# A transformer's step loop: ScalarE makes the reciprocal lengths between two copies, and VectorE gates ahead of its sums of squares

## The chip, the cores and the metric

The kernel runs on one core of a Trainium2 chip. The core has five engines with their own in-order queues: TensorE (PE), VectorE (DVE), ScalarE (ACT), GpSimd (POOL) and SyncE (SP), which here only issues transfers. They meet by semaphores. The metric is the device time in microseconds (us) of one execution; the median of three runs is 2576.67 us (2573.55 to 2577.73).

## The reference, cut to what matters

The input x is 2048 tokens of width 128, all in float32. Two layers follow each other:

- layer 0 adds to x a causal attention of 16 heads and a mixture of 8 experts (two are picked for each token), both on the normalised x;
- layer 1 adds to the result a state space branch (a short convolution, rates, and a scan over the tokens with 16 states for each of 256 channels) and a branch of six transformer layers, both on the normalised x.

The change lies in the six transformer layers. Each computes, on tokens shifted by one in half of the channels:

```
q, k, v = split(x @ Wqkv)                    # 16 heads of 64
q = q / max(|q|, 1e-12) * q_scale            # the lengths: one per token and head
k = k / max(|k|, 1e-12) * k_scale
q, k = rotary(q), rotary(k)
x = x + softmax(mask(8 q k^T)) v @ Wo        # windows of 32, each sees itself and the one before
xn = (x - mean) / sqrt(var + 1e-5) * g + b
a, gate = split(xn @ W1 + b1)                # 341 wide each
x = x + (a * gelu(gate)) @ W2 + b2
```

## The kernel before

After layer 0 the core goes through one loop of 96 steps (6 transformer layers of 16 tiles of 128 tokens, `NTILE` = 96), software-pipelined over all layers, with seven steps more to drain it. Each engine has its own function with its own copy of the loop (`transformer_pe`, `transformer_act`, `transformer_dve`, `transformer_pool`, `transformer_sp`), and the order inside a step is written out by hand. The values are never formed: the heads' probabilities weigh the rows of x (the "mixed values"), and one product with the folded Wv Wo follows.

What happens to one tile runs over several steps. In step n:

- TensorE projects q and k of tile n+2 (L1447), forms the attention output of tile n-1 (L1550, from both halves of the mixed values), turns q and k rows of tile n+1 (L1455), does a third of a feed-forward product (L1564, L1565) or a product down (L1571) and four transposes (L1556), the scores of tile n+1 (L1471, L1462) in two halves with the mixing of tile n between them (L1512).
- ScalarE (`transformer_act`) copies the two halves of the mixed values of tile n-1 out of PSUM (`mix_out`, L1785), squares q and k of tile n+2 (L1729), takes the 16 exponentials of tile n (L1778), copies turned x, q and k (L1739, L1757, L1765, L1767), makes the decays of the scan (L472), and then gelu for a third of four tiles' hidden rows (`gelu`, L1800), between two loads of its function tables (L1903, L1913). Last it makes the reciprocal lengths of tile n+2: logarithm L1718 and exponential L1722 (`lengths`), which wait for VectorE's clamped sums (semaphore `squares`).
- VectorE (`transformer_dve`) takes the maxima of tile n (`top`, L1932), the rotary products of tile n+2 (`rotate`, L1952, one for q and one for k), the sum of tile n-1 (L1969), the softmax weights (L1936, L1938, L1940) and their transpose (L1944), then sums the squares of tile n+2 (`sum_squares`, L1958) and clamps them (L1962), does its share of the convolution in steps 4 to 14 (L1182), the gate (`gated`, L2018: the product of one PSUM bank with gelu's output), and the scan (L2034).
- GpSimd (`transformer_pool`) refines the reciprocal lengths by a Newton step (`better`, L2126 to L2132), scales q and k of tile n+1 by them (`normal`, L2139), does the scan's inputs and outputs (L481, L509, L511) and the rotary additions of tile n+2 (L2119, L2120); in one of four steps also the layer norm of four tiles (L2143 to L2151).

`forward_step` sets what the feed-forward does: steps with n % 4 = 3, 0, 1 have the first, second and third part of the product up with gelu and gate; steps with n % 4 = 2 have none, but the transposes and the product down. The scan's 64 later units are in four blocks of 16 steps: steps 23 to 38, 41 to 56, 59 to 74 and 77 to 92 (a unit's decay and scan are issued at the end of the step before).

PSUM's eight banks are four pairs. `pair_table` hands them on in a ring: q of tile n+3 goes to the pair of step n's feed-forward part, which is free when the gate has read it (semaphore `hv`), k of tile n+3 to the pair of the first half of the mixed values (`mixT`, first copy), and the attention output of step n+1 to the pair of the second half.

Of the kernel before, what the change touches and what calls it, by code (L numbers as in the profile page):

```python
# [41 lines left out]
NTILE = L * NT  # L42
# [1107 lines left out]
def variance_dve(k):  # L1150

    V, s, st = k.ve, k.sem, k.st[:, :, 0:NTH]
    V.wait_ge(s("ln_squared"), 1)
    V.tensor_reduce(st[:, 2, :], k.sqr, X_AXIS, ALU.add).then_inc(s("v"), k.v.up())
    V.wait_ge(s("v"), k.v.n)
    V.tensor_scalar(st[:, 3, :], st[:, 2, :], 1.0 / P, EPS, ALU.mult, ALU.add).then_inc(s("v"), k.v.up())
    V.wait_ge(s("v"), k.v.n)
    V.reciprocal(st[:, 0, :], st[:, 3, :]).then_inc(s("v"), k.v.up())
    V.wait_ge(s("v"), k.v.n)
    V.tensor_scalar(st[:, 2, :], st[:, 0, :], -EPS, 1.0 + EPS, ALU.mult, ALU.add).then_inc(s("ln_var"), 1)  # L1160
# [89 lines left out]
def forward_step(n):  # L1250

    what = (("up1", 8), ("up2", 9), ("turn_normal", 6), ("up0", 7))[n % 4]
    m = (n - what[1]) // 4
    return (what[0], m) if 0 <= m < NTILE // 4 else (None, m)
# [450 lines left out]
def transformer_act(k):  # L1705
    A, s, ps = k.ac, k.sem, k.ps

    def pair(*key):
        p = k.pair[key]
        return ps[:, 2 * p:2 * p + 2, :]  # L1710
# [4 lines left out]
    def lengths(n):  # L1715

        A.wait_ge(s("squares"), n + 1)
        A.activation(k.lnx[:], k.sx[:, n % 2, :], ACT.Ln, scale=65536.0).then_inc(s("lnx"), 1)  # L1718
        A.wait_ge(s("lnx"), n + 1)
        if n >= 2:  # L1720
            A.wait_ge(s("normal_k"), n - 1)
        A.activation(k.rn[:, n % 2, :], k.lnx[:], ACT.Exp, scale=-0.5, bias=k.ln256[:]).then_inc(s("rn"), 1)  # L1722

    def square(what, n):
        w = 0 if what == "q" else 1
        A.wait_ge(s(what + "_mm"), n + 1)
        if n:
            A.wait_ge(s("summed"), n)
        A.activation(k.sq[:, w, :], flat(what, n), ACT.Square).then_inc(s("sq_" + what), 1)  # L1729
# [51 lines left out]
    def mix_out(n, i):  # L1781
        A.wait_ge(s("mixed"), 2 * n + i + 1)
        if n:
            A.wait_ge(s("fin_mm"), n)
        A.activation(k.mixT[:, :, 2 * i:2 * i + 2, :].rearrange("p c w q -> p w c q"), pair(f"mix{i}", n).rearrange("p w (c q) -> p w c q", q=WIN), ACT.Copy).then_inc(s("mixT"), 1)  # L1785
# [20 lines left out]
    def norm_squared():  # L1806
        A.wait_ge(s("ln_centred"), 1)
        A.activation(k.sqr, k.xn[:, NTH:NT, :], ACT.Square).then_inc(s("ln_squared"), 1)
# [54 lines left out]
    for n in range(LAST_STEP):  # L1863
        if 1 <= n <= NTILE:
            mix_out(n - 1, 0)
            mix_out(n - 1, 1)
        if n + 2 < NTILE:
            square("q", n + 2)
            square("k", n + 2)
        if n < NTILE:  # L1870
            probs(n, 0)
            probs(n, 1)
        if n == 0:
            norm_squared()
        if n + 3 < NTILE:
            turned_input(n + 3)
        if n in FOLD_STEPS:
            folded_share(n)
        for u in units(n):
            if u // NS + 1 < NCH:  # L1880
                unit_state(k, u)
        if new_frame(n + 1) and n + 1 < NTILE:
            halo_turned(n + 1)
        if n + 1 < NTILE:
            queries_out(n + 1)
            keys_out(n + 1)
        for u in units(n + 1):
            A.wait_ge(s("chunk"), 32 * (u // NS - NCH // 2 + 1))
            unit_decay(k, u)
        if n in IN_LATE:  # L1890
            projected_in("late", n, IN_LATE[n])
        if n == FACTOR_STEP:
            factors(n)
        if n in RATE_STEPS:
            rates(n, RATE_STEPS[n])
        for place, l, half in FOLDS.get(n, ()):
            folded(place, n, l, half)
        what, m = forward_step(n)
        if what == "turn_normal":
            normal_turned(m)  # L1900
        elif what:
            if n < NTILE:
                A.preload_act_table_set("gelu_and_others")  # L1903
            gelu(m, int(what[2]))
        if n == HAT_STEP:
            turned_hat(0)
            turned_hat(1)
        if n in IN_EXTRA:
            projected_in("extra", n, IN_EXTRA[n])
        if n in SILU_STEPS:  # L1910
            convolved(SILU_STEPS[n])
        if what and what != "turn_normal" and n < NTILE - 1 or IN_EXTRA.get(n, 0) >= ET:
            A.preload_act_table_set("natural_log_exp_and_others")  # L1913
        if n + 2 < NTILE:
            lengths(n + 2)
        if n in RATE_STEPS:
            softplus(RATE_STEPS[n])


def transformer_dve(k):  # L1920
# [94 lines left out]
    def gated(m, j):  # L2015
        o, w = FCH[j]
        V.wait_ge(s("gelu"), 3 * m + j + 1)
        V.scalar_tensor_tensor(k.hv[0:w, j, :], pair("extra", 4 * m + 7 + j)[0:w, 1, :], k.colA[0:w, m // (NT // 4) % 2, 5 + j:6 + j], k.hv[0:w, j, :], ALU.add, ALU.mult).then_inc(s("hv"), 1)  # L2018
# [26 lines left out]
    for n in range(LAST_STEP):  # L2045
        taps = conv_share(n)
        for a, t in taps[:2]:
            conv_dve(k, a, t)
        if n < NTILE:
            top(n)  # L2050
        if n == 0:
            centre_dve(k)
        if n + 2 < NTILE:
            rotate("q", n + 2)
            rotate("k", n + 2)
        if 1 <= n <= NTILE:
            finish(n - 1)
        if n in CHUNK_OUT:
            chunk_sum(CHUNK_OUT[n])
        if n < NTILE:  # L2060
            weigh(n)
        if n == 0:
            variance_dve(k)
        if n + 2 < NTILE:
            sum_squares(n + 2)
        for a, t in taps[2:]:
            conv_dve(k, a, t)
        if n == 1:
            normal_dve(k)
            V.wait_ge(s("turned"), TURNED + 2)  # L2070
            V.memset(k.hv[DH:DH + WIN, 2, :], 1.0)
            V.tensor_copy(k.xs[:, NTH + 1:NT + 1, :], k.xn[:, NTH:NT, :]).then_inc(s("copied"), 1)
        what, m = forward_step(n)
        if what and what != "turn_normal":
            gated(m, int(what[2]))
        if n == NTILE + 6:
            down_last()
        elif n % 4 == 2 and m >= 1:
            down(m - 1)
        if n % 4 == 1 and 0 <= (n - 5) // 4 < NTILE // 4:  # L2080
            measure((n - 5) // 4)
        if n == NTILE + 1:
            normalise_last()
        if n == NTILE + 3:
            add_last()
        elif n == NTILE + 4:
            add_layer(0)
            add_layer(1)
        elif n == NTILE + 5:
            add_layer(2)  # L2090
        for u in units(n + 1):
            scan(u)
# [343 lines left out]
```

## Time and profile before

| What | Value |
|---|---|
| median of three runs | 2576.67 us |
| profiled execution | 2573.51 us, its span 2571.7 us |
| PE busy | 2374.6 us (92% of the span) |
| DVE busy | 2266.8 us (88%) |
| POOL busy | 1949.9 us (76%) |
| ACT busy | 1851.5 us (72%) |
| mean granted TensorE clock | 0.981 |
| the step loop | step 0 begins at 953 us, the last exponential of a tile at 2531 us |

The profile is one execution on the chip. Busy time counts work instructions of an engine, not its waits. Times in the rows are microseconds from the span's start; in groups of instructions "mean ns" is nanoseconds. The slices of the page show TensorE's granted clock at nine tenths or more of full speed throughout.

### The profile page before, as it was taken

The numbers are of one execution on the slowest core, as the hardware profiler recorded it, in microseconds if no ns is written. First come the engines' busy times: TensorE is split into PE (matmuls) and PEld (weight loads), VectorE is DVE, ScalarE is ACT, GpSimd is POOL, SyncE is SP. The second block draws the span as 40 slices with busy tenths as digits, with TensorE's granted clock in tenths as the row PEclk, the third lists the DMA queues.
The fourth block names the chain that finished last, engine by engine and source line by source line (L and its number), as shares of the span: only waits on it lengthen the run. The fifth ranks groups of instructions, "written<-read, shape, count | busy, mean of one in ns | idle before, by whom it ended". The sixth has DMA issues, their size and how long they took to land. (4 is left out here: it accounts for less than half of the span.)

```text
span 2571.7 us, 67534 instructions
## 1 busy us (share of the span) xinstructions
PE 2374.6 (92%) x26742; PEld 1428.9 (56%) x26742; DVE 2266.8 (88%) x2520; ACT 1851.5 (72%) x4113; POOL 1949.9 (76%) x1768
## 2 busy tenths in 40 slices
PE   7999999899898869899889999999999999999997
PEld 4444443333333336566566666666667666666665
DVE  6778879879999988999769999899999999899994
ACT  4566555556666647777778888888888888888883
POOL 2441147947888857777578999899999999999991
PEclk9999999999999989999999999999999999999999
DMA  3000000002333310300211112111211221111101
GB/s 109 9 9 11 9 7 7 15 24 57 57 60 57 62 33 8 98 14 12 67 44 43 32 51 46 40 35 49 46 40 30 45 59 33 37 35 33 30 17 40
DMA packets 171112, 97.22 MB, mean 38 GB/s; under 512 B 97156, under 2 KB 167792, under 8 KB 169264
## 3 DMA queue, kind: packets, MB, share of 16 engines
q1 hardware_dynamic: 170799, 92.91, 15.9%
q8 instruction: 215, 3.52, 0.6%
q14 instruction: 98, 0.79, 0.1%
HBM read 66.91 MB, written 7.08 MB: 29 GB/s over the span
## 5 line engine op out<-in xcount | busy, mean ns | idle before, releaser
L608 PE MATMUL ps<-xnT,qp 128*128 128x512 f32 (+3 forms) x1280 | 564.5, 562 | 11.2 <-ACT prob L833 11.1
L833 ACT ACTIVATE prob<-ps,mneg,shift 128x1024 f32<-128x1024 f32 (+7 forms) x384 | 366.6, 955 | 285.1 <-DVE mneg L728 284.6
L1952 DVE TENSOR_TENSOR area<-ps,tab 128x2048 f32<-128x2048 f32 x192 | 430.7, 2284 | 59.1 <-ACT area L1729 33.7
L728 DVE TENSOR_REDUCE mneg<-ps 128x1 f32<-128x1024 f32 (+7 forms) x384 | 340.7, 888 | 73.2 <-PE ps L608 72.8
L1447 PE MATMUL ps<-wqk,area 128*128 128x512 f32 x768 | 360.8, 613 | 28.3 <-DVE area L2018 23.4
L736 DVE STREAM_TRANSPOSE area<-prob 128x1024 f32<-128x1024 f32 (+7 forms) x384 | 352.1, 917 | 31.1 <-ACT prob L833 24.9
L2139 POOL TENSOR_TENSOR area<-area,rn 128x1024 f32<-128x1024 f32 x192 | 371.6, 1957 | 7.5
L1550 PE MATMUL ps<-wvo,area 128*128 128x128 f32 x3072 | 364.4, 277 | 3.3 <-ACT area L1785 3.3
L1550 PEld LDWEIGHTS ps<-wvo,area 128*128 128x128 f32 x3072 | 354.8, 193 | 22.3 <-issue 13.1
L608 PEld LDWEIGHTS ps<-xnT,qp 128*128 128x128 f32 x1280 | 222.8, 196 | 202.9 <-issue 175.3
L1778 ACT ACTIVATE ps<-ps,nmxl 128x64 f32<-128x64 f32 x1536 | 322.5, 344 | 4.1 <-DVE nmxl L1932 4.0
L1729 ACT ACTIVATE area<-ps 128x1024 f32<-128x1024 f32 x192 | 196.7, 1025 | 103.3 <-PE ps L1447 103.2
L956 POOL TENSOR_TENSOR vb<-staged,own 128x1024 f32<-128x1024 f32 x48 | 90.9, 1894 | 226.7 <-PE ps L677 219.1
L2119 POOL TENSOR_TENSOR area<-area 128x512 f32<-128x512 f32 x192 | 252.7, 1316 | 5.1 <-DVE area L1952 4.6
L2120 POOL TENSOR_TENSOR area<-area 128x512 f32<-128x512 f32 x192 | 253.7, 1321 | 0.0
L1447 PEld LDWEIGHTS ps<-wqk,area 128*128 128x128 f32 x768 | 139.4, 192 | 182.6 <-issue 130.6
L1455 PE MATMUL ps<-ident,area 128*128 128x128 f32 x1536 | 194.0, 278 | 36.7 <-POOL area L2139 24.5
L1958 DVE TENSOR_REDUCE ss<-area 128x32 f32<-128x2048 f32 x96 | 215.5, 2245 | 0.0
L1455 PEld LDWEIGHTS ps<-ident,area 128*128 128x128 f32 x1536 | 173.2, 143 | 47.2 <-issue 31.2
L1462 PEld LDWEIGHTS ps<-kT,area 64*32 64x32 f32 x12288 | 146.0, 105 | 84.2 <-issue 79.2
L1785 ACT ACTIVATE area<-ps 128x1024 f32<-128x1024 f32 x192 | 184.5, 1011 | 10.0 <-PE ps L1512 9.9
L677 PE MATMUL ps<-area,vb 128*32 128x256 f32 (+7 forms) x3072 | 167.4, 325 | 2.9 <-POOL vb L956 2.9
(279 smaller groups left out, 4366.2 us busy)
## 6 DMA issues: line engine op xcount, KB each, us to landing
xe<-bc_scratch SPq DMA_DIRECT2D x128, 128.0 KB, 3.7
area<-bc_scratch SPq DMA_DIRECT2D x128, 128.0 KB, 4.1
staged<-values_scratch SPq DMA_DIRECT2D x192, 32.0 KB, 1.9
wqk<-lwqk_dram SPq DMA_DIRECT2D x6, 1024.0 KB, 6.4
xp<-xc SPq DMA_DIRECT2D x96, 48.0 KB, 2.6
xc<-xs SPq DMA_DIRECT2D x96, 32.0 KB
wvT<-lwvT_dram SPq DMA_DIRECT2D x6, 512.0 KB, 7.8
wo<-lwo_dram SPq DMA_DIRECT2D x6, 512.0 KB, 9.4
```

The lines of the kernel that those rows point to most:

```text
L608: mm = E.matmul(ps[:, r + o // 512, 0:w], k.qp[:, group % 2, i * P:(i + 1) * P], k.xnT[:, k0 + o:k0 + o + w], start=o // 512 != masked, st ...
L728: V.tensor_reduce(k.mneg[:, U:U + 1], of, X_AXIS, ALU.max, negate=True).then_inc(s("top"), 1)
L736: V.transpose(k.probT[x][:, i * STRIDE[x]:i * STRIDE[x] + nk], k.prob[:, U % 2, 0:nk]).then_inc(s("prob_turned"), 1)
L833: A.activation(k.prob[:, U % 2, 0:nk], ps[:, r:r + 2, :].rearrange("p a b -> p (a b)")[:, 0:nk], ACT.Exp, bias=k.mneg[:, U:U + 1], scale=k ...
L1447: mm = E.matmul(to[:, c, :], k.xcT[:, n % 4, :], k.wqk[l % 2][:, at + 512 * c:at + 512 * (c + 1)], start=True, stop=True)
L1455: mm = E.transpose(to[:, j // 4, j % 4 * P:(j % 4 + 1) * P], k.rot[:, n % 2, w, 0, j * P:(j + 1) * P], k.ident[:])
L1550: mm = E.matmul(to[:, 0, 0:P], k.mixT[:, c, :, :].rearrange("p w q -> p (w q)"), k.wvo[:, l % 2, c, :], start=c == 0, stop=c == H - 1, ski ...
L1778: ins = A.activation(here, here, ACT.Exp, bias=k.nmxl[:, n % 2, 8 * o + j:8 * o + j + 1])
L1952: V.tensor_tensor(k.rot[:, n % 2, w, :, :].rearrange("p c (h d) -> p c h d", d=DH), bcast(heads(what, n), 1, 2), bcast(k.tab[:, n % FRAME, ...
L2119: G.tensor_tensor(a[:, :, 0:DH // 2], a[:, :, 0:DH // 2], b[:, :, DH // 2:DH], ALU.add)
L2120: G.tensor_tensor(a[:, :, DH // 2:DH], a[:, :, DH // 2:DH], b[:, :, 0:DH // 2], ALU.add).then_inc(s("added_" + what), 1)
L2139: G.tensor_tensor(of, of, bcast(k.rn[:, n % 2, H * w:H * (w + 1)], 2, DH), ALU.mult).then_inc(s("normal_" + what), 1)
```

## The change

Two calls move; no instruction is added or removed.

- In ScalarE's loop, `lengths` of tile n+2 stood at the end of step n (behind gelu and the second table load, and ahead of `softplus` in the two steps that have it). It now stands in step n+1, between the two copies of the mixed values. Tile 0 and tile 1 are made ahead of the loop as before.
- In VectorE's loop, `gated` stood behind `sum_squares` and the convolution's last taps. It now stands ahead of `sum_squares`, right behind the softmax weights and their transpose.

```diff
@@ transformer_act, the loop
     for n in range(LAST_STEP):
         if 1 <= n <= NTILE:
             mix_out(n - 1, 0)
+            if n + 1 < NTILE:
+                lengths(n + 1)
             mix_out(n - 1, 1)
...
         if what and what != "turn_normal" and n < NTILE - 1 or IN_EXTRA.get(n, 0) >= ET:
             A.preload_act_table_set("natural_log_exp_and_others")
-        if n + 2 < NTILE:
-            lengths(n + 2)
         if n in RATE_STEPS:
             softplus(RATE_STEPS[n])
@@ transformer_dve, the loop
         if n == 0:
             variance_dve(k)
+        what, m = forward_step(n)
+        if what and what != "turn_normal":
+            gated(m, int(what[2]))
         if n + 2 < NTILE:
             sum_squares(n + 2)
         for a, t in taps[2:]:
...
-        what, m = forward_step(n)
-        if what and what != "turn_normal":
-            gated(m, int(what[2]))
         if n == NTILE + 6:
             down_last()
```

## Rows read from the trace of the kernel before

**Rows 1.** The page, parts 1 and 5: busy us, share; a group's busy us, mean ns.
```profile
PE 2374.6 (92%) x26742; PEld 1428.9 (56%) x26742; DVE 2266.8 (88%) x2520; ACT 1851.5 (72%) x4113; POOL 1949.9 (76%) x1768
...
L1729 ACT ACTIVATE area<-ps 128x1024 f32<-128x1024 f32 x192 | 196.7, 1025 | 103.3 <-PE ps L1447 103.2
```
**Rows 2.** Stretches: length, busy PE PEld DVE ACT POOL, clock, DMA; first, last scan block.
```profile
1365.94:1622.00 256.06, 246.20 (x3541) 172.47 (x3541) 242.87 (x240) 217.73 (x507) 242.00 (x232) 1.00 0.19 43
...
2238.41:2496.38 257.97, 242.78 (x3518) 169.72 (x3516) 248.80 (x240) 215.39 (x487) 243.10 (x232) 1.00 0.16 32
```
**Rows 3.** The waits: who waited for whom, us, times, longest.
```profile
POOL rt L2126 <- ACT rn L1722: 91.7, 31, 7.3
...
ACT lnx L1718 <- DVE sx L1962: 74.6, 59, 4.1
...
PE ps L1447 <- DVE area L2018: 23.4, 33, 1.2
```
**Rows 4.** Timeline of VectorE, steps 64 to 67: start, duration, line, operation, idle before.
```profile
2042.47 1.19 DVE L1962 TENSOR_SCALAR sx<-ss 128x32 f32<-128x32 f32 x1
...
2055.23 1.25 DVE L1944 STREAM_TRANSPOSE area<-area 128x1024 f32<-128x1024 f32 x1
2056.40 2.24 DVE L1958 TENSOR_REDUCE ss<-area 128x32 f32<-128x2048 f32 x1
...
2060.88 1.36 DVE L2034 TENSOR_TENSOR_SCAN acc<-acc,last 128x256 f32<-128x256 f32 x2
...
2086.65 1.25 DVE L1944 STREAM_TRANSPOSE area<-area 128x1024 f32<-128x1024 f32 x1
...
2090.77 0.75 DVE L2018 SCALAR_TENSOR_TENSOR area<-ps,area 128x512 f32<-128x512 f32 x1 [0.27 <-ACT area L1800]
```
**Rows 5.** Timeline of ScalarE, steps 64 to 69.
```profile
2040.77 0.69 ACT L1800 ACTIVATE area<-ps,area 128x512 f32<-128x512 f32 x1
...
2043.70 0.23 ACT L1718 ACTIVATE lnx<-sx 128x32 f32<-128x32 f32 x1 [0.94 <-DVE sx L1962]
...
2044.19 1.92 ACT L1785 ACTIVATE area<-ps 128x1024 f32<-128x1024 f32 x2
...
2049.03 3.36 ACT L1778 ACTIVATE ps<-ps,nmxl 128x64 f32<-128x64 f32 x16
...
2056.99 0.68 ACT L1800 ACTIVATE area<-ps,area 85x512 f32<-85x512 f32 x1
...
2086.64 1.02 ACT L1765 ACTIVATE kT<-ps 128x1024 f32<-128x1024 f32 x1 [0.84 <-PE ps L1455]
...
2090.05 0.69 ACT L1800 ACTIVATE area<-ps,area 128x512 f32<-128x512 f32 x1
...
2104.62 0.69 ACT L1800 ACTIVATE area<-ps,area 128x512 f32<-128x512 f32 x1
...
2120.84 0.68 ACT L1800 ACTIVATE area<-ps,area 85x512 f32<-85x512 f32 x1
```
**Rows 6.** Timeline of GpSimd, steps 64 to 67.
```profile
2042.34 1.29 POOL L2119 TENSOR_TENSOR area<-area 128x512 f32<-128x512 f32 x1
...
2060.25 0.27 POOL L2126 TENSOR_TENSOR rt<-rn,sx 128x32 f32<-128x32 f32 x1
...
2081.63 3.77 POOL L2139 TENSOR_TENSOR area<-area,rn 128x1024 f32<-128x1024 f32 x2
```
**Rows 7.** Timeline of TensorE, steps 64 to 67.
```profile
2044.37 3.70 PE L1447 MATMUL ps<-wqk,area 128*128 128x512 f32 x8 [1.06 <-DVE area L2018]
...
2085.55 1.06 PE L1455 MATMUL ps<-ident,area 128*128 128x128 f32 x8 [0.80 <-POOL area L2139]
```
**Rows 8.** Timeline of VectorE in steps 8, 16 and 85.
```profile
1099.58 0.29 DVE L1969 TENSOR_TENSOR ys<-xs,ps 128x128 f32<-128x128 f32 x1 [0.49 <-PE ps L1550]
...
1245.99 0.75 DVE L2018 SCALAR_TENSOR_TENSOR area<-ps,area 128x512 f32<-128x512 f32 x1 [1.59 <-ACT area L1800]
...
2383.31 2.96 DVE L2034 TENSOR_TENSOR_SCAN acc<-acc,last 128x256 f32<-128x256 f32 x2
```

## Prediction before the run

> **What bounds the kernel now.** I read the page's busy shares first, then the stretches of the second layer's steps, then the waits, then the timelines of one group of four steps. The shares say that no engine is idle enough to be left out: TensorE 92%, VectorE 88%, GpSimd 76%, ScalarE 72% [rows 1]. The 96 steps of the layers differ. Four blocks of 16 steps, which also carry the scan, take 256 to 259 us each, and in the first of them VectorE works 242.9 of 256.1 us, TensorE 246.2 and GpSimd 242.0 [rows 2]. Those blocks are a ring of four nearly full engines that wait for each other by tenths of a microsecond. A change of order there can't save much work, it can only move waits. The reader is to see three in the list of waits [rows 3]: ScalarE waits 74.6 us (59 times) for VectorE's clamped sums before it makes the lengths, GpSimd 91.7 us for the lengths, TensorE 23.4 us for VectorE's gate.
>
> In the settled part of a block four steps repeat. I take steps 65 to 69. Step 67 gates the first third of the hidden width, 68 the second, 69 the third, 66 nothing. Measured between the ends of ScalarE's gelu (G, start plus duration), 65 to 67 takes 2057.67 to 2090.74, so 33.07; 67 to 68 takes 14.57; 68 to 69 takes 16.21; the group 63.85 [rows 5].
>
> **Part 1, the lengths between the two copies.** The two ScalarE instructions stay (0.49 us together, from 2043.70 to 2044.19) and so do the two copies (1.92 for both, 0.93 of them until the next can start) [rows 5]. Before, the pair of copies stands behind the wait for the clamped sums, 0.94 us in step 64 [rows 5]. After, the first copy is done in that wait. If the sums came at the old time this would give up to 0.94 us to the second copy, the squares and the exponentials behind it, and cost GpSimd the same at the lengths. It hides nothing where the sums are there already. No instruction crosses a DMA queue; SP is not touched, and its loads of the next tiles still go by the mixing products and the layer's ends.
>
> In steps 17 and 18 the lengths also come behind the softplus instructions instead of ahead of them. I cost that at nothing: GpSimd there is held by the rates. If that cover fails it is about 3.6 us, once or twice.
>
> **Part 2, the gate ahead of the sums.** No instruction is added, but the gate waits for gelu, and VectorE is in order: sums, clamp, scan and the next maximum queue behind it. In step 65 the transpose ends at 2056.48 and gelu at 2057.67, so VectorE would stand 1.2 us; in step 67 the transpose ends at 2087.90 and gelu at 2090.74, so 2.84 us, of which 0.27 is idle today [rows 4, 5]. Taken without any feedback a group would lose 1.2 + 1.2 + 2.6 = 5.0 us. That is the upper bound of the harm. The lower bound is a gain: TensorE's projections wait 1.06 us for the gate in step 64 [rows 7] and less in the other steps; with the gate at once this is gone, and the sum over the kernel is 23.4 us [rows 3].
>
> With feedback, I follow the three stretches, counting from G.
> The clamped sums now end at G + 0.04 + 0.67 (gate) + 2.27 (sums, [rows 4]) + 0.25 (clamp) = G + 3.2 at the latest, and the lengths 0.6 later, at G + 3.85.
> - Third gate to first gate, 33.07 us. GpSimd begins on the lengths of this step at 2060.25, G + 2.58, and is idle nowhere until the normal of step 67's keys ends at 2085.40; TensorE waits 0.80 us for that, ScalarE's copy of the keys 0.84 for TensorE, and gelu follows with no idle time [rows 5 to 7]. GpSimd now begins at G + 3.85. So gelu of 67 comes 1.27 us later. VectorE gets to its gate before it and waits. +1.27.
> - First gate to second, 14.57. The chain is new: clamped sums G + 3.2, lengths 0.49, second copy 0.93, two squares 1.85 (1.025 each, less what two neighbours overlap; [rows 1]), then from the first exponential to the end of gelu 8.64 (2049.03 to 2057.67, [rows 5]). Together 15.2. +0.64.
> - Second gate to third, 16.21. Here TensorE's projection of the keys is last: before, it ended 6.61 us after G (2044.37 + 3.70 against 2041.46). TensorE was free at 2044.37 - 1.06 = 2043.31, G + 1.85 [rows 7]; its mixing hangs on VectorE's transpose, which now stands up to 0.6 nearer to gelu. So it begins at G + 2.5 and ends at G + 6.2. -0.4.
> Group: 63.85 + 1.27 + 0.64 - 0.4 = 65.4, or 1.5 us more.
>
> How long VectorE's clamp and scans take depends on GpSimd. The clamp of step 64 took 1.19 us and ended at 2043.66, as GpSimd's add ended at 2043.63; the two scans of step 65 took 1.36 us, those of step 85, beside GpSimd's normal, 2.96 [rows 4, 6, 8]. The change lets GpSimd stand for up to 1.3 us behind the lengths just when the clamp runs, so I take 0.25 for it instead of up to 1.19. Against that, in the third gate's step the scans move to G + 4.5, onto GpSimd's normals; 1.6 us more for VectorE, which this stretch covers (VectorE's transpose of step 67 is 2.84 us early today), and up to 0.65 for GpSimd, which it doesn't.
> The Trainium skill, "SBUF — State Buffer", section "Who interferes with whom", says that the port pair shared by VectorE and GpSimd is an exclusive lock held for a whole instruction. The rows of step 64 agree. By that rule alone each scan put onto a normal costs the full rest of it, and the group would be 66.0 instead of 65.4.
>
> **Sum over the kernel.** First and last block are 257.0 us in the mean, a group of 64.3 rather than 63.85, since each block starts unsettled [rows 2]; against this mean 65.4 is +1.1. I take +1.25, between 1.1 and 1.5, for 16 groups: +20. Steps 7 to 13 carry the convolution on VectorE, which alone bounds them; there ScalarE, which has no decays to make, catches up after one step, and the 0.49 us that VectorE waits in step 8 for TensorE's output product goes as the projections start earlier [rows 8]: -3 over six such steps. Steps 16, 17, 19: gelu is late anyway (VectorE idle 1.59 us before the gate in step 16, [rows 8]), the sums behind it come 2 us later, and the maximum waits for TensorE after that: +2 for the three. The six steps between blocks: 0.5 each, +3. Sum +22. The profiled execution took 2573.51 us (span 2571.7, 1.8 around it); it would become 2595.5. The median of the runs before, 2576.67, lies 3.2 above it, so 2598.7, say 2598.
>
> **The rivals.**
> A. ScalarE and TensorE gain more than VectorE loses. It needs gelu to come to the transpose in every step; then VectorE has no wait and runs at its own work. For it: today's waits of TensorE for the gate, and ScalarE's 74.6 us behind the clamp, both of which go. A group's busy time is 60.7 us on VectorE, 60.5 on GpSimd and 61.6 on TensorE (a quarter of the first block's, [rows 2]). No ring gets down to that; halfway between 61.6 and 64.3 is 63.0, and 16 groups give -21: 2555 at best. Half of it, 2566, is the case's own value. Against it: GpSimd is at 242 of 256 us and starts later at each lengths.
> B. Nothing moves beyond 0.2%: losses at the first gate, where VectorE waits, come back at the second and third. 2577. It needs the first stretch to gain elsewhere 1.3 us.
> C. VectorE's wait is not taken back: gelu is set by TensorE's row transposes and not by the exponentials, so that the full wait stands at each gate. Half of the 5.0 us bound: 2.5 x 16 + 2 = +42, 2619; this case decides from the point where gelu ends over 1.5 us behind the transpose in second and third gates too. The lock on the normals leads the same way, +10.
> D. The move of the lengths does nothing because the clamped sums are late in any case by the gate; then part 1 is worth only the first copy, as in my sum, and the result is the forecast's.
>
> **How the numbers follow.** About 5 us (0.2%) is what this kernel's measurement can tell from nothing. My forecast with D, between 2583 and 2610: 0.52. C, above 2610: 0.19. A, below 2571.5: 0.19. B: 0.10. Slower in all 0.71, same 0.10, faster 0.19. The range is to leave out half of A and the tail of C: 2566 to 2622. The forecast's own range is 2583 to 2610.
>
> **What the changed kernel's profile would show.** VectorE's gate starts within 0.05 us of gelu's end, with 0.3 to 3 us of idle time before it, most in first-gate steps; the wait of TensorE's projection for the gate is gone. The lengths wait about 1 us for the clamp behind the first copy. GpSimd waits some 1 us for the lengths in two of four steps of a block, where today it waits hardly at all. The four-step group is 65 to 66 us. I am wrong if the group is 63.85 or less, if VectorE's idle before the gate is under 0.3 us in first-gate steps, or if GpSimd's start on the lengths is not later against gelu.

## The result: 0.8% slower, and the profile after

The changed kernel takes 2595.36 us (median of 4 runs, 2592.94 to 2595.97). The kernel before took 2575.11 on the same chip (4 runs, 2573.04 to 2577.73). The ratio is 1.0083, 95% interval 1.0068 to 1.0097. The profiled execution has a span of 2591.1 us, before 2571.7. The forecast was 2598.

The page of the changed kernel, part 1 (busy us, share, instructions) and one group of part 5:
```profile
PE 2380.7 (92%) x26742; PEld 1429.0 (55%) x26742; DVE 2238.5 (86%) x2520; ACT 1848.9 (71%) x4113; POOL 1932.1 (75%) x1768
...
L1729 ACT ACTIVATE area<-ps 128x1024 f32<-128x1024 f32 x192 | 191.2, 1020 | 52.5 <-PE ps L1447 52.3
```
Every engine has the same number of instructions as before [rows 1]. VectorE and GpSimd are even busy for less (2238.5 against 2266.8 us, 1932.1 against 1949.9), TensorE for 6 us more, and the profiled execution is 19.4 us longer: the loss is waiting. ScalarE's squares (L1729) waited 103.3 us in all for TensorE's projections and now wait 52.5, so one thing did get faster as the change has it.

The waits of the changed kernel: who waited for whom, us, times, longest:
```profile
POOL rt L2126 <- ACT rn L1722: 151.7, 72, 8.3
...
DVE area L2018 <- ACT area L1800: 116.7, 71, 6.6
...
ACT lnx L1718 <- DVE sx L1962: 62.9, 67, 4.8
...
PE ps L1455 <- DVE area L1952: 31.8, 45, 2.1
```
TensorE's 23.4 us for the gate [rows 3] are gone from this list. In their place VectorE waits 116.7 us (71 times) for gelu ahead of its gate, where before it waited 18.8 (18 times); GpSimd's wait for the lengths has grown from 91.7 us (31 times) to 151.7 (72 times), and TensorE's for VectorE's rotary products from 11.4 to 31.8. So 98 us of new standing time on an 86% busy engine went with 19 us of kernel. Which of these waits cost something can't be read off this list.

Stretches of the changed kernel, columns as in [rows 2]; first and last scan block:
```profile
1365.33:1628.47 263.14, 249.98 (x3542) 172.98 (x3540) 235.16 (x239) 216.86 (x504) 238.60 (x232) 0.99 0.18 42
...
2258.43:2518.75 260.32, 244.40 (x3517) 169.20 (x3516) 236.37 (x240) 214.56 (x485) 240.62 (x233) 1.00 0.15 31
```
The four blocks grew by 7.1, 4.9, 4.3 and 2.3 us (from 256.06, 258.75, 255.84, 257.97), together 18.6 of the 19.4. The granted clock is 0.99 to 1.00 in all of them, before and after, so hardly any of it is TensorE's clock. VectorE works 7.7 us less in the first block and 12.4 less in the last: its scans take 898 ns in the mean instead of 1070 and its clamps 431 instead of 502, since they meet GpSimd's instructions less often, and that buys nothing here.

Now one group of four steps, the same one as in [rows 4 to 7]. VectorE's timeline in steps 65, 67 and 68 (start, duration, line, operation, idle before):
```profile
2072.03 0.74 DVE L2018 SCALAR_TENSOR_TENSOR area<-ps,area 85x512 f32<-85x512 f32 x1 [1.15 <-ACT area L1800]
2072.70 2.27 DVE L1958 TENSOR_REDUCE ss<-area 128x32 f32<-128x2048 f32 x1
2075.00 0.18 DVE L1962 TENSOR_SCALAR sx<-ss 128x32 f32<-128x32 f32 x1
...
2076.29 1.36 DVE L2034 TENSOR_TENSOR_SCAN acc<-acc,last 128x256 f32<-128x256 f32 x2
...
2101.99 1.25 DVE L1944 STREAM_TRANSPOSE area<-area 128x1024 f32<-128x1024 f32 x1
...
2106.13 0.75 DVE L2018 SCALAR_TENSOR_TENSOR area<-ps,area 128x512 f32<-128x512 f32 x1 [2.89 <-ACT area L1800]
...
2109.11 0.45 DVE L1962 TENSOR_SCALAR sx<-ss 128x32 f32<-128x32 f32 x1
2109.47 1.38 DVE L2034 TENSOR_TENSOR_SCAN acc<-acc,last 128x256 f32<-128x256 f32 x2
2110.78 1.19 DVE L1932 TENSOR_REDUCE nmxl<-ps 128x16 f32<-128x1024 f32 x1
2112.08 4.49 DVE L1952 TENSOR_TENSOR area<-ps,tab 128x2048 f32<-128x2048 f32 x2
...
2121.88 0.75 DVE L2018 SCALAR_TENSOR_TENSOR area<-ps,area 128x512 f32<-128x512 f32 x1 [1.15 <-ACT area L1800]
```
ScalarE's timeline in the same steps:
```profile
2071.31 0.68 ACT L1800 ACTIVATE area<-ps,area 85x512 f32<-85x512 f32 x1
...
2073.30 1.02 ACT L1785 ACTIVATE area<-ps 128x1024 f32<-128x1024 f32 x1
2075.22 0.23 ACT L1718 ACTIVATE lnx<-sx 128x32 f32<-128x32 f32 x1 [0.89 <-DVE sx L1962]
2075.48 0.32 ACT L1722 ACTIVATE rn<-lnx,ln 128x32 f32<-128x32 f32 x1
...
2105.41 0.69 ACT L1800 ACTIVATE area<-ps,area 128x512 f32<-128x512 f32 x1
...
2110.98 1.01 ACT L1729 ACTIVATE area<-ps 128x1024 f32<-128x1024 f32 x1
...
2112.79 3.36 ACT L1778 ACTIVATE ps<-ps,nmxl 128x64 f32<-128x64 f32 x16
...
2117.76 1.03 ACT L1765 ACTIVATE kT<-ps 128x1024 f32<-128x1024 f32 x1 [0.41 <-PE ps L1455]
...
2121.16 0.69 ACT L1800 ACTIVATE area<-ps,area 128x512 f32<-128x512 f32 x1
```
GpSimd's timeline, from the lengths of step 65 to the normal of step 67's keys:
```profile
2075.88 0.25 POOL L2126 TENSOR_TENSOR rt<-rn,sx 128x32 f32<-128x32 f32 x1 [1.19 <-ACT rn L1722]
2076.20 0.25 POOL L2128 TENSOR_TENSOR rt<-rt,rn 128x32 f32<-128x32 f32 x1
2076.54 0.47 POOL L2130 TENSOR_SCALAR rt<-rt 128x32 f32<-128x32 f32 x1
2077.10 0.59 POOL L2132 TENSOR_TENSOR rn<-rn,rt 128x32 f32<-128x32 f32 x1
...
2097.00 3.76 POOL L2139 TENSOR_TENSOR area<-area,rn 128x1024 f32<-128x1024 f32 x2
```
And TensorE's two transposes of the keys, of steps 67 and 68:
```profile
2100.91 1.07 PE L1455 MATMUL ps<-ident,area 128*128 128x128 f32 x8 [0.80 <-POOL area L2139]
...
2116.63 1.09 PE L1455 MATMUL ps<-ident,area 128*128 128x128 f32 x8 [0.71 <-DVE area L1952]
```
With G the end of gelu, as in the prediction, these lines give a table of stretches from one gelu's end to the next, good to 0.02 us. A runs from the third gate's step to the first's (65 to 67), B from the first to the second (67 to 68), C from the second to the third (68 to 69).

| | A | B | C | group | VectorE idle before the gate, 65 / 67 / 68 |
|---|---|---|---|---|---|
| before | 33.07 | 14.57 | 16.21 | 63.85 | 0 / 0.27 / 0 |
| forecast | 34.34 | 15.21 | 15.81 | 65.4 | 1.2 / 2.8 / 1.2 |
| after | 34.11 | 15.75 | 15.48 | 65.33 | 1.15 / 2.89 / 1.15 |

For A the reader is to see GpSimd's start at 2075.88, G + 3.89 (G is 2071.99), where it was G + 2.58 [rows 6]. From there to the end of the keys' normal GpSimd takes 24.88 us, 25.15 before. For B the chain goes over three engines. VectorE's gate, sums and clamp hold up ScalarE's lengths, behind which come the second copy and the square of the queries, which ends at 2111.99. VectorE's rotary products wait for that square in the kernel: they start 0.09 us behind it, at 2112.08, when VectorE's own maximum has ended 0.11 us before. TensorE's transpose then waits 0.71 us for the rotary products, and ScalarE's copy of the keys 0.41 us for TensorE.

### The profile page after: what moved, and what is told of

The parts are those of the page before. It is cut to its first block and busy times, and to the rows that moved or that the text cites. A ratio compares the mean times of both kernels' runs of the same rounds, so it can differ in the third digit from the quotient of the medians.

```text
span 2591.1 us, 67534 instructions
## 1 busy us (share of the span) xinstructions
PE 2380.7 (92%) x26742; PEld 1429.0 (55%) x26742; DVE 2238.5 (86%) x2520; ACT 1848.9 (71%) x4113; POOL 1932.1 (75%) x1768
## 3 DMA queue, kind: packets, MB, share of 16 engines
q8 instruction: 215, 3.52, 0.6%
## 5 line engine op out<-in xcount | busy, mean ns | idle before, releaser
L2139 POOL TENSOR_TENSOR area<-area,rn 128x1024 f32<-128x1024 f32 x192 | 362.2, 1908 | 7.5
L1778 ACT ACTIVATE ps<-ps,nmxl 128x64 f32<-128x64 f32 x1536 | 321.8, 346 | 10.5 <-DVE nmxl L1932 10.4
L1455 PE MATMUL ps<-ident,area 128*128 128x128 f32 x1536 | 202.2, 279 | 62.1 <-DVE area L1952 31.8
L2119 POOL TENSOR_TENSOR area<-area 128x512 f32<-128x512 f32 x192 | 249.7, 1301 | 3.8 <-DVE area L1952 3.4
L2120 POOL TENSOR_TENSOR area<-area 128x512 f32<-128x512 f32 x192 | 250.2, 1303 | 0.0
L1729 ACT ACTIVATE area<-ps 128x1024 f32<-128x1024 f32 x192 | 191.2, 1020 | 52.5 <-PE ps L1447 52.3
L1462 PE MATMUL ps<-kT,area 64*32 64x64 f32 x12288 | 164.9, 225 | 4.4 <-issue 3.6
```

The source lines that it names most:

```text
L1455: mm = E.transpose(to[:, j // 4, j % 4 * P:(j % 4 + 1) * P], k.rot[:, n % 2, w, 0, j * P:(j + 1) * P], k.ident[:])
L1462: mm = E.matmul(to[WIN * w:WIN * (w + 1), o, j * DH:(j + 1) * DH], k.qT[o * DH:(o + 1) * DH, j, WIN * w:WIN * (w + 1)], k.kT[o * DH:(o + 1 ...
L1778: ins = A.activation(here, here, ACT.Exp, bias=k.nmxl[:, n % 2, 8 * o + j:8 * o + j + 1])
L2120: G.tensor_tensor(a[:, :, DH // 2:DH], a[:, :, DH // 2:DH], b[:, :, 0:DH // 2], ALU.add).then_inc(s("added_" + what), 1)
L2139: G.tensor_tensor(of, of, bcast(k.rn[:, n % 2, H * w:H * (w + 1)], 2, DH), ALU.mult).then_inc(s("normal_" + what), 1)
```

## Experiments

The kernel before took 2575 us (four runs) in the first comparison and 2581 to 2582 in those of the experiments on three chips, where its 51 runs lie between 2566.8 and 2591.2. So I compare ratios, each with the kernel before on the same chip, and stretches within traces. The table has all twelve runs; A, B, C are of the steps 65 to 69. The changed kernel itself (1.0083) was not run again beside them.

| run | median us | ratio to before (95%) | A | B | C | group |
|---|---|---|---|---|---|---|
| e1 lengths alone | 2580.2 | 0.9993 (0.9982 to 1.0005) | 33.26 | 14.55 | 16.21 | 64.02 |
| e2 gate alone | 2640.7 | 1.0228 (1.0210 to 1.0246) | 34.11 | 16.65 | 16.39 | 67.15 |
| e3 gate ahead, third only | 2596.3 | 1.0048 (1.0031 to 1.0065) | 34.12 | 14.55 | 16.22 | 64.88 |
| e4 gate ahead, first only | 2580.1 | 0.9993 (0.9981 to 1.0005) | 33.31 | 15.73 | 15.42 | 64.46 |
| e5 gate ahead, second only | 2567.4 | 0.9950 (0.9938 to 0.9963) | 33.28 | 14.55 | 15.72 | 63.56 |
| e6 after, no refinement | 2654.9 | 1.0285 (1.0271 to 1.0300) | 38.41 | 15.49 | 15.49 | 69.39 |
| e7 before, no refinement | 2614.0 | 1.0123 (1.0105 to 1.0142) | 36.13 | 15.02 | 15.44 | 66.59 |
| e8 gate between sums and clamp | 2564.2 | 0.9940 (0.9926 to 0.9953) | 33.34 | 15.13 | 15.15 | 63.61 |
| e9 the same, second only | 2562.0 | 0.9926 (0.9907 to 0.9946) | 33.16 | 14.55 | 15.38 | 63.09 |
| e10 the same, second and third | 2561.8 | 0.9924 (0.9908 to 0.9940) | 33.43 | 14.55 | 15.37 | 63.35 |
| e11 after, light row norm | 2559.4 | 0.9916 (0.9898 to 0.9935) | 33.15 | 15.49 | 15.48 | 64.12 |
| e12 e6 with two scans earlier | 2579.3 | 0.9999 (0.9988 to 1.0010) | 33.14 | 15.49 | 15.48 | 64.10 |

### The two parts by themselves

e1 keeps `gated` at its old place; e2 keeps `lengths` at its old place:
```diff
@@ e1, against after, transformer_dve
-        what, m = forward_step(n)
-        if what and what != "turn_normal":
-            gated(m, int(what[2]))
         if n + 2 < NTILE:
             sum_squares(n + 2)
@@ e2, against after, transformer_act
-            if n + 1 < NTILE:
-                lengths(n + 1)
...
+        if n + 2 < NTILE:
+            lengths(n + 2)
```


> The lengths between the two copies, the gate at its old place behind the sums. My theory (the loss is the gate's, through the lateness of the clamped sums against gelu): the settled group of four stays within 0.4 us of 63.85, steps 0 to 6 keep the 2.5 us that they gained in the changed kernel, in all 2565 to 2577 us against 2575. Rival (the lengths behind a copy hold GpSimd and cost by themselves): group at 64.5 or more, GpSimd idle before the lengths in two of four steps, in all 2583 or more.

> The gate ahead of the sums, the lengths at their old place at the end of the step. My theory: the lengths are made at the same time after gelu as in the changed kernel (some 3.8 us), but the first copy stands behind the wait and both copies, the squares and the exponentials come 0.9 us later in each gate step; group 67 to 68, in all 2610 to 2635. Rival (the lengths' move is what costs): the group is 64 to 65, in all 2575 to 2585.

Measured: the lengths alone change nothing that can be told (0.9993), the gate alone costs 2.3% (2640.7 us, above the 2635 that I had expected at most). The waits of e1:
```profile
PE ps L1447 <- DVE area L2018: 32.4, 46, 1.2
```
TensorE still waits for the gate, more than before. ScalarE's wait for the clamp, 74.6 us before, is down to 6.4 in e1, and that buys nothing. e1's first stretch is 0.2 us longer, since the lengths of step 65 come at G + 2.81 rather than 2.07 and GpSimd starts at G + 2.89 rather than 2.58. Beside VectorE's gate ahead, though, the move of the lengths is worth 65.33 - 67.15 = -1.8 us a group, 0.90 in B and 0.91 in C. The timelines of ScalarE and VectorE in e2 behind the gelu of step 67, which ends at 2138.25, show why:
```profile
2141.73 0.23 ACT L1718 ACTIVATE lnx<-sx 128x32 f32<-128x32 f32 x1 [2.18 <-DVE sx L1962]
...
2142.22 1.92 ACT L1785 ACTIVATE area<-ps 128x1024 f32<-128x1024 f32 x2
2144.03 1.02 ACT L1729 ACTIVATE area<-ps 128x1024 f32<-128x1024 f32 x1
```
```profile
2145.14 4.49 DVE L1952 TENSOR_TENSOR area<-ps,tab 128x2048 f32<-128x2048 f32 x2 [1.03 <-issue]
```
The lengths start at G + 3.48, as in the changed kernel (G + 3.49). ScalarE stands 2.18 us ahead of them with both copies queued behind, and 1.16 us in the changed kernel, where one copy is done in the wait. A copy keeps ScalarE for 0.93 us until the next instruction can start, and the squares and VectorE's rotary products come that much later: VectorE stands 1.03 us, and its products again start 0.09 us behind the first square's end. Between the two comparisons this is 1.45% (1.0228 against 1.0083), some 37 us. The harm is the gate's, and the move of the lengths pays back part of it.

### Which of the three gates costs

e3, e4 and e5 are the changed kernel with `gated` ahead of the sums in one kind of step only, and at its old place in the others:
```diff
@@ transformer_dve, e3 (e4: n % 4 == 3; e5: n % 4 == 0)
-        if what and what != "turn_normal":
+        gate = what and what != "turn_normal"
+        if gate and n % 4 == 1:
             gated(m, int(what[2]))
...
+        if gate and not (n % 4 == 1):
+            gated(m, int(what[2]))
```


> As the changed kernel, but the gate is ahead of the sums only in steps with n % 4 = 1 (third part of the hidden width); in the others it is behind them. My theory: stretch from the end of the third gelu to the end of the first (65 to 67) keeps its loss, 34.1 against 33.07, since the lengths of this step start GpSimd's unbroken run late; the two other stretches go back to about 14.6 and 16.2; group 64.9, in all 2585 to 2590. Rival (the loss is the time that VectorE stands before the gate, 1.15 of 5.2 us a group in this step): 22% of the loss, 2579.

> As the changed kernel, but the gate is ahead of the sums only in steps with n % 4 = 3 (first part). VectorE will stand 2.6 to 2.9 us there. My theory: the stretch before it (65 to 67) is back at 33.1, as VectorE's standing costs nothing to what sets gelu; the stretch behind it (67 to 68) has 15.7; the third stays 16.2 or gains a little; group 64.5 to 65, in all 2583 to 2590. Rival (VectorE's standing is lost time): the group loses at least half of the 2.6 us and the stretch 65 to 67 is longer as well; 2592 or more.

> As the changed kernel, but the gate is ahead of the sums only in steps with n % 4 = 0 (second part). From the runs so far: stretch from third to first gelu 33.1 to 33.3 (lengths of the third step early again), first to second 14.55, second to third 15.5 as in the changed kernel (there the gate no longer stands behind a clamp that waits for GpSimd). Group 63.2 to 63.4 against 63.85 to 64.05: 4 to 12 us less than before, ratio 0.995 to 0.999. Rival (the 0.7 us gained in the third stretch were the other side of the loss in the second, since the first gate was late): third stretch 16.2, group 64 or more, ratio 1.000 to 1.004.

Measured: A and B follow each its own gate alone. A is 34.12 in e3 and 33.3 in e4 and e5; B is 15.73 in e4 and 14.55 in the others. Taken alone the third gate costs (1.0048; 2596.3 us, more than the 2585 to 2590 expected), the first costs nothing net (0.9993), and the second gains (0.9950). Of the gates of e4:
```profile
2101.00 0.75 DVE L2018 SCALAR_TENSOR_TENSOR area<-ps,area 128x512 f32<-128x512 f32 x1 [3.04 <-ACT area L1800]
...
2117.78 0.34 DVE L1962 TENSOR_SCALAR sx<-ss 128x32 f32<-128x32 f32 x1
2118.03 0.74 DVE L2018 SCALAR_TENSOR_TENSOR area<-ps,area 128x512 f32<-128x512 f32 x1
```
VectorE stands 3.04 us ahead of the first gate, and A stays at 33.31 (33.26 in e1, which has the gate at its old place, and 33.07 before). So its standing time is not what makes A long, which was the rival I had put up against GpSimd's late start. The same lines explain C: the gate of step 68 is at its old place, behind a clamp of 0.34 us that ends at G + 1.42. Before, that clamp ended at G + 2.20. C fell to 15.42, as much as with the gate ahead in every step (15.48); in e1, where the clamp takes 1.20 us again, it is 16.21. My expectation for e4 had the stretches right and missed this gain of 0.8 us, so its total was 0.1 to 0.4% too high.

The effects in the group add up to +1.0 on top of before (e1 +0.2, then +0.9, +0.4, -0.5), against +1.5 of the change. The stretches say where the other 0.5 comes from. The gain in C is there in e4 (15.42) and in e5 (15.72), and the changed kernel has it once (15.48), so the sum counts it twice. In the changed kernel, against e1, the third gate costs 0.85 us a group in A, the first 1.20 in B, and C gives back 0.73: the gain in C that makes up for part of the first gate's cost in e4 can't be had twice.

The times of whole kernels are no test of this. Taken from e1 the ratios of the three are worth +14, 0 and -11 us, with e1's own -2 some +1, against +21 of the change; the spans of the profiled executions add up to +21.8 against +19.4, and that is luck, as e1 and e4 spread over 12 and 11 us from run to run. In the four scan blocks alone the same sum gives +9.9 against +18.6.

### Is it GpSimd, and what is the shared port worth

If GpSimd's unbroken run of work sets A, a shorter run must shorten it. e6 and e7 take three small instructions per step from it, out of the refinement of the reciprocal lengths, in the changed kernel and in the one before. e11 leaves the refinement and makes the row norm light:
```diff
@@ e6 (on after) and e7 (on before), better
-        G.tensor_tensor(z, y, x, ALU.mult).then_inc(s("g"), k.g.up())
...
-        G.tensor_tensor(y, y, z, ALU.mult).then_inc(s("rn_better"), 1)
+        G.tensor_tensor(z, y, x, ALU.mult).then_inc(s("rn_better"), 1)
@@ e11 (on after), normalise
-        for t in range(4):
-            ins = G.tensor_scalar(k.xf[:, t, :], ..., ALU.subtract, ALU.mult)
-        ins.then_inc(s("xf_normal"), 1)
+        G.memset(k.xf[:, 0:1, :], 0.5)
...
+        G.memset(k.xf[:, 3:4, :], 0.5).then_inc(s("xf_normal"), 1)
```


> The changed kernel with GpSimd's refinement of the reciprocal lengths left out: one of its four small instructions stays, the lengths are used as ScalarE made them, so the last digits of the output differ. It shortens GpSimd's run from the third gelu to the first by 1.5 to 2.5 us and nobody else's. My theory (GpSimd's late start sets the stretch 65 to 67): the stretch falls from 34.1 by 0.8 to 1.0 us, the idle time of TensorE ahead of the turned keys, where TensorE's own work takes over; group 64.3 or so. Rival (VectorE's chain of gate, sums and rotary products sets it): the stretch stays 34.1.

> The kernel before with the same refinement left out. GpSimd has slack here in two of four steps and VectorE stands 0.3 us at most before the gate. My theory: stretch 65 to 67 falls by up to 0.8 us too, as TensorE waits 0.80 us for GpSimd's scaled keys, but VectorE is the full engine and the group falls by 0.3 to 0.5 us only, 63.4 to 63.6. Rival (VectorE's order sets both kernels): nothing in either.

Both expectations were wrong: with less work the kernels became 2.9% and 1.2% slower, and A grew to 38.41 and 36.13. VectorE's two scans in the third gate's step of e6, together 4.61 us:
```profile
2112.87 2.37 DVE L2034 TENSOR_TENSOR_SCAN acc<-acc,last 128x256 f32<-128x256 f32 x1
2115.16 2.32 DVE L2034 TENSOR_TENSOR_SCAN acc<-acc,last 128x256 f32<-128x256 f32 x1
```
and GpSimd's two products that scale the queries and the keys (the "normals"):
```profile
2112.79 1.90 POOL L2133 TENSOR_TENSOR area<-area,rn 128x1024 f32<-128x1024 f32 x1
2114.65 2.29 POOL L2133 TENSOR_TENSOR area<-area,rn 128x1024 f32<-128x1024 f32 x1
```
In the changed kernel the two scans run beside GpSimd's four small instructions (1.36 us, 2076.29 to 2077.65, ahead of the normals at 2077.77). Two of these take 0.47 and 0.59 us there and 0.22 and 0.25 in step 66, so the scans cost GpSimd 0.6 us and themselves nothing. In e6 the normals start at 2112.79, 0.08 us ahead of the scans. The first scan ends 0.55 us after the first normal, the second 0.55 us after the second, and the second normal takes 0.39 us longer than the first: the first scan got in between the two normals, and each scan cost VectorE the rest of one. In e7 the scans of that step take 4.41 us. The Trainium skill ("SBUF — State Buffer", section "Who interferes with whom") says that VectorE and GpSimd share a port pair as an exclusive lock held for a whole instruction. The trace agrees, with 2.37 and 2.32 us for scans of 0.7.

e12 separates the cause from the missing instructions: it is e6 with the two scans moved ahead of the statistics in the third gate's step.
```diff
@@ e12, on e6, transformer_dve
+        if n % 4 == 1:
+            for u in units(n + 1):
+                scan(u)
...
-        for u in units(n + 1):
-            scan(u)
+        if n % 4 != 1:
+            for u in units(n + 1):
+                scan(u)
```


> The changed kernel, where GpSimd fills the four normalised tiles with a constant instead of normalising them (the feed-forward works on constants, the output is another). This takes about 2 us out of GpSimd's run in one of four steps, behind the scaled queries and keys and so behind VectorE's scans of that step, which the refinement's removal had disturbed. My theory (GpSimd's run sets stretch 65 to 67): it falls from 34.1 by 0.8 to 1.0 us to where TensorE's own work or VectorE takes over; group 64.3 to 64.6, 12 to 16 us less than the changed kernel. Rival (VectorE's order sets the stretch): 34.1 stays.

> The changed kernel without the refinement of the lengths, as before, and with VectorE's two scans ahead of the layer norm statistics in steps with n % 4 = 1. There the scans took 4.61 us beside GpSimd's two long scaling instructions instead of 1.36. If it is the shared port, held by GpSimd's instruction and then by the next, the scans now run before GpSimd starts, about 1.4 us, the step after is 16.5 instead of 20.3 us, and the kernel is near 2590, 60 us less than without this. Rival (leaving out the refinement slows something else, as TensorE's clock): the scans move but the step stays near 20.

VectorE and then GpSimd in e12, step 65:
```profile
2072.27 1.38 DVE L2034 TENSOR_TENSOR_SCAN acc<-acc,last 128x256 f32<-128x256 f32 x2
```
```profile
2073.78 3.76 POOL L2137 TENSOR_TENSOR area<-area,rn 128x1024 f32<-128x1024 f32 x2
```
The scans are back at 1.38 us, A is 33.14 (32.8 in most other groups), and the kernel is 0.9999 of before, where e6 was 1.0285. So the loss of e6 was the meeting of scans and normals, with the price in TensorE's clock that it brought (last section), and moving two instructions took it back. e11 answers the first question: with the refinement in place and GpSimd's run shorter by 2.5 us, A falls from 34.11 to 33.15 (32.8 in most others), so in the changed kernel GpSimd sets A; below 33.15 something else does. The whole kernel gained more than the 12 to 16 us that I expected of it: 36 us by the medians; by the traces 22 of it lie in the four scan blocks. I didn't follow the rest.

### A better place for the gate

The gain in C came with TensorE's projection and an unobstructed clamp, the loss in A and B with VectorE waiting ahead of the sums. e8 puts the gate behind the sums and ahead of the clamp, so that the sums cover the wait for gelu:
```diff
@@ sum_squares(n, gate), between tensor_reduce and the clamp
+        if gate:
+            gated(*gate)
@@ transformer_dve, e9 (e8: in all; e10: n % 4 != 3)
+        between = gate and n + 2 < NTILE and n % 4 == 0
-            sum_squares(n + 2)
+            sum_squares(n + 2, gate if between else None)
...
+        if gate and not between:
+            gated(*gate)
```


> As the changed kernel, but in every step the gate stands between the sum of squares and its clamp. Gelu ends 1.1 us behind the transpose in second and third gate steps, the sums take 2.24, so VectorE does not stand there; in the first gate step it stands 0.6. The gate is not behind the clamp's wait for GpSimd any more. My theory: clamped sums end 1.2 to 2.0 us after gelu, stretches 33.1 to 33.4, 14.6 to 14.8, 15.4; group 63.1 to 63.6, ratio 0.994 to 0.999. Rival (what counts is only that the lengths come not later than before): they come up to 0.7 us later than before at the third gate, stretch 65 to 67 is 33.7, group 64 or more, ratio 1.000 to 1.004.

> Lengths between the copies; the gate between the sum and its clamp only in steps with n % 4 = 0, at the old place behind both in the others. My account of the stretches: third to first gelu as with the old gate, 33.1 to 33.3; first to second 14.55; second to third 15.15, since the projections no longer wait for a gate behind a stalled clamp. Group 62.8 to 63.1, the steps before 16 a little slower than with the gate between everywhere; ratio 0.990 to 0.995. Rival (the stretches are not independent: what the second gate step gains the next stretch gives back at GpSimd): group 63.5 or more, ratio 0.995 to 0.998.

> The same, with the gate between sum and clamp in second and third gate steps, behind both in first ones (n % 4 = 3), where gelu ends 2.8 us behind the transpose and a gate in between makes VectorE stand 0.6 to 0.9 us. My account: 33.3 to 33.7, 14.55, 15.15; group 63.1 to 63.4; ratio 0.991 to 0.995. Rival as for the other: 63.6 and 0.994, no better than the gate between everywhere.

VectorE in e10 (line numbers of the gate and below are two higher there), second gate of a group (step 64):
```profile
2039.35 2.24 DVE L1958 TENSOR_REDUCE ss<-area 128x32 f32<-128x2048 f32 x1
2041.52 0.74 DVE L2020 SCALAR_TENSOR_TENSOR area<-ps,area 128x512 f32<-128x512 f32 x1
2042.17 0.66 DVE L1964 TENSOR_SCALAR sx<-ss 128x32 f32<-128x32 f32 x1
```
No wait stands ahead of the gate; gelu has ended beneath the sums. All three beat the kernel before: 0.9940, 0.9926, 0.9924, with overlapping intervals, so that none of the three is shown to be the best. e8's B is 15.13 against 14.55 in e9 and e10: in the first gate's step gelu is so late that the sums don't cover it (idle 0.86 us).
The waits of e10:
```profile
POOL rt L2130 <- ACT rn L1722: 111.0, 45, 8.2
...
DVE area L2020 <- ACT area L1800: 20.0, 21, 4.2
...
ACT lnx L1718 <- DVE sx L1964: 8.8, 15, 4.1
```
VectorE's wait for gelu is 20.0 us instead of 116.7 in the changed kernel, ScalarE's for the clamp 8.8 instead of 62.9, and GpSimd's 111.0 instead of 151.7.

One loss is left in most of these versions. Step 18 takes 28.6 us before, 26.9 in the changed kernel and 28.7 in e8, but 28.9 in e3, 29.9 in e1, and 31.3 to 31.5 in e4, e5, e9 and e10. The work is the same; the granted clock is not. Step 18 in e8 and in e9 (columns as in [rows 2]):
```profile
1260.17:1288.91 28.74, 21.73 (x242) 15.63 (x243) 12.80 (x12) 15.83 (x32) 20.47 (x19) 0.88 0.03 6
```
```profile
1265.83:1297.22 31.39, 25.11 (x241) 17.55 (x241) 12.80 (x11) 15.44 (x32) 20.06 (x19) 0.73 0.02 5
```
In both TensorE stands 4.78 us for GpSimd's scaled queries and then has a clock below 1.00. In e8 the step's mean is 0.88, as before (0.88), in e9 0.73, and TensorE is busy 3.4 us longer there with the same products. Why the clock comes back later in e9 than in e8 stays open. A kernel with e8's order in that step and e9's elsewhere was not tried.

## Why the prediction was right, step by step

**The shape was right: little work saved, waits moved.** The instruction counts are equal, VectorE's busy time fell by 28 us, and the time rose by 19.

**Stretch A, +1.27: right (+1.04).** GpSimd starts at G + 3.89 (forecast 3.85), its run to the keys' normal is 0.27 us shorter than before, which the forecast didn't have, and the keys' normal, TensorE's transpose (still 0.80 us of wait) and gelu follow as written. e3 alone keeps the loss; e4 and e5 take it away; e11 shortens GpSimd's run and A with it. Shown.

**Stretch B, +0.64: mis-sized (+1.18), and the chain is partly another.** ScalarE's exponentials start at G + 6.69 where my sum had about 6.5 (its terms add up to 15.1, not the 15.2 that I wrote), so this half is some 0.2 short. Then gelu ended 9.06 us after their start instead of 8.64, since ScalarE's copy waited 0.41 for the transposed keys. The path by lengths, second copy and first square was right. Behind the square I followed ScalarE's exponentials and left out the branch through VectorE's rotary products: they start behind the square, end at G + 10.5, and TensorE's transpose waits for them.

**Stretch C, -0.4: right in sign, too small (-0.73), and credited to the wrong cause.** I had TensorE's projection begin at G + 2.5 because VectorE's transpose and with it the mixing stand up to 0.6 us nearer to gelu. The mixing came 0.07 us nearer and the projection began at G + 1.85, as soon as TensorE was free. e4 has the gate at its old place and reaches 15.42. What had held the gate back before was the clamp ahead of it, 1.19 us beside GpSimd's add [rows 4, 6]; with it at 0.34, as in e4, a gate behind it holds the projection back by 0.2 us only.

**The three errors cancel.** A is 0.23 less than forecast, B 0.54 more, C 0.33 less. That the group came out at 65.33 for 65.4 is luck in that part; the signs were all right.

**The clamp at 0.25 instead of 1.19: right** (0.18 in steps 64, 65 and 68, 0.45 in 67). **The scans onto the normals, 1.6 us more: did not come,** nor did the 66.0 us of the account in which each scan pays the rest of a normal. They took 1.36 us; I had not seen that GpSimd's refinement stands ahead of the normals and leaves room for them. e6 shows what had been at stake: 4.61 us, and 2% of the kernel against the changed one.

**The sum.** Four blocks: +18.6, forecast +20. Between blocks (39 to 41, 57 to 59, 75 to 77): +1.4, +0.7, +2.3 = +4.4, forecast +3. Steps 7 to 13, forecast -3 through earlier projections, gave -1.1: step 7, where VectorE waits 0.88 us ahead of the gate, went from 16.43 to 18.26, while 9, 11 and 13 became 0.6 to 1.6 shorter. Steps 14 and 15 gave that back, so most of this gain failed. Steps 16, 17 and 19, forecast +2: +0.5. The lengths behind the softplus instructions, which I costed at nothing, cost nothing (step 17 +0.1, step 18 -1.7). Not forecast: step 0 starts 1.6 us later, steps 0 to 7 take 1.3 less, 93 to 95 0.9 more, and what follows step 95 takes 3.9 less. These small terms nearly cancel, and the total of +22 against +19.4 owes something to that, too.

**The rivals.** B, nothing beyond 0.2%, is refuted by the result. C, the full wait standing at each gate (+42), is refuted: VectorE stands 5.2 us in a group and loses 1.5, and e4's 3.04 us of standing leave A alone. Its mechanism, gelu set by TensorE's row transposes and not by the exponentials, did come in B, where it is worth 0.41 us. The size of its loss was close to what e2 does (1.0228), where the lengths stay behind. A, TensorE's gain exceeding VectorE's loss, is refuted for the change as a whole, and holds for the second gate taken alone (e5, 0.9950). D, part 1 worth only the first copy, is what came: 0.90 us in B and 0.91 in C beside the gate ahead, and nothing that can be told by itself (e1). Of the signs named for the profile one was off: GpSimd waits for the lengths in three steps of the group (1.29, 1.19 and 0.73 us), not in two.

## What to carry to other kernels

In a ring of nearly full engines, measure stretches between one recurring event and ask in each which chain ends last; a sum of an engine's waits says little (98 us of new waits went with a loss of 19 us, and in e4 a wait of 3 us in every group cost the kernel nothing that could be told). When a wait is moved ahead in an in-order queue, first look for work that can stand ahead of it: 0.93 us of copy ahead of the lengths was worth 1.8 us a group beside the early gate (and nothing without it), and 2.2 us of sums ahead of the gate turned 0.8% slower into 0.6% faster (e8). A placement that helps in one kind of step can harm in another: try it by kind of step, and don't add up what each gives alone, since two of them can earn the same gain.

## What the runs showed of the hardware that was not expected

- Taking three small GpSimd instructions (0.7 to 1.3 us of work) out of every step made a kernel 2.0% slower (e6 against the changed kernel, 1.0285 and 1.0083): the two 128x256 scans of VectorE then took 4.61 us beside two back-to-back GpSimd products instead of 1.36 us. Beside a row of short GpSimd instructions with 0.07 to 0.09 us between them the scans lost nothing and GpSimd 0.6 us; beside the two 1.9 us products each scan lost the rest of one.
- In e6 TensorE's granted clock fell after 3.52 us without work. Its transposes and two stretches (columns as in [rows 2]):
```profile
2120.85 1.97 PE L1455 MATMUL ps<-ident,area 128*128 128x128 f32 x8 [3.52 <-DVE area L1952]
```
```profile
2105.00:2113.00 8.00, 7.45 (x161) 3.79 (x160) 6.75 (x14) 6.52 (x11) 7.11 (x8) 1.00 0.74 236
...
2120.00:2128.00 8.00, 6.93 (x36) 6.53 (x37) 7.90 (x8) 5.12 (x16) 7.92 (x8) 0.57 0.30 52
```
The clock is at 1.00 in the first and 0.57 in the second, most of the stretch at the 1.2 GHz level; eight transposes took 1.97 us instead of 1.07. So this wait brought a second price, as TensorE's 4.78 us ahead of its transposes do in step 18 (clock 0.88 and 0.73, above). In the changed kernel TensorE's waits in the group are at most 1.11 us and its clock there is 1.00.
